# A two-layer graph kernel on one core: first two graphs' attention in four-pass products, first graph's side work divided anew

## The reference

```python
h = einsum('bni,oi->bno', x, W_fc)                    # 16 graphs, 512 nodes, 256 features; o = 32
f1, f2 = h @ a1, h @ a2                               # a1, a2: halves of W_attn
scores = leaky_relu(f1[:, :, None] + f2[:, None, :], 0.2)
attn = softmax(where(adj == 0, -1e9, scores), axis=2) # adj: 512 x 512 of 0/1 per graph
x = layernorm(x + elu(attn @ x))
xn = x / sqrt(max(sum(x * x), 1e-12))
x = layernorm(x + ((xn @ xn.T) @ adj) @ x)
```

## Time and profile before

| | |
|---|---|
| time, median of 3 runs (lowest to highest) | 339.91 us (339.04 to 342.74) |
| the profiled execution's own time | 339.95 us |
| its span, first to last instruction | 338.1 us |
| mean granted TensorE clock | 0.990 |
| busy: PE, PEld, DVE, ACT, POOL | 318.5, 301.3, 287.0, 293.3, 210.3 us |

### The profile page before, as it was taken

The page is one execution under the profiler, slowest core; times in us unless marked ns, Lnnn a source line. Parts: engine busy times, 40 slices in busy tenths (PEclk is TensorE's granted clock), DMA queues, the critical chain, the costliest instruction groups (busy, mean ns, idle before and its releaser), DMA issues.

```text
span 338.1 us, 7382 instructions
## 1 busy us (share of the span) xinstructions
PE 318.5 (94%) x2418; PEld 301.3 (89%) x2418; DVE 287.0 (85%) x1013; ACT 293.3 (87%) x610; POOL 210.3 (62%) x238
## 2 busy tenths in 40 slices
PE   6778899999989999999999999999999999999992
PEld 3577799989889999999999999999999998998881
DVE  2889999999788989989898989989898989856635
ACT  1589989999699999999999999999999999993561
POOL 4340493877447666675967676676958676665623
PEclk9979999999999999999999999999999999999998
DMA  8633461560715455264464454363464462210122
GB/s 237 201 88 104 123 186 25 166 186 8 240 37 156 124 151 163 71 181 124 126 181 130 127 157 156 81 186 111 138 174 128 131 177 67 65 62 0 44 73 74
DMA packets 33494, 41.93 MB, mean 124 GB/s; under 512 B 1168, under 2 KB 25264, under 8 KB 33456
## 3 DMA queue, kind: packets, MB, share of 16 engines
q0 software_dynamic: 16416, 24.64, 26.6%
q1 hardware_dynamic: 16944, 16.78, 15.9%
q10 hardware_dynamic: 96, 0.03, 0.0%
HBM read 33.06 MB, written 8.39 MB: 123 GB/s over the span
## 4 chain that ended last, share of the span: by engine, by line
PE 79%; DVE 10%; POOL 4%; issue 3%; ACT 2%; DMA 1%; POOLq 0%; ACTq 0%; DVEq 0%
PE ps_l L1208 14%; PE ps_l L1168 9%; PE ps_l L1169 8%; PE ps_h L1138 8%; PE ps_h L1139 7%; PE ps_h L1140 7%; PE ps_probT L1122 6%; PE ps_l L1194 4%; PE ps_l L1196 4%; PE ps_l L1195 4%; PE ps_l L1180 4%; PE ps_f L1111 2%; DVE score L453 1%; DVE product L432 1%; DMA wfc<-w_fc 1%
## 5 line engine op out<-in xcount | busy, mean ns | idle before, releaser
L1138 PE MATMUL ps_h<-x_hi,probT_hi 128*128 128x256 f32 x256 | 78.8, 308 | 7.6 <-POOL x_lo L263 2.3
L1139 PE MATMUL ps_h<-x_lo,probT_hi 128*128 128x256 f32 x256 | 72.0, 281 | 0.0
L1140 PE MATMUL ps_h<-x_hi,probT_lo 128*128 128x256 f32 x256 | 72.0, 281 | 0.0
L1168 PE MATMUL ps_l<-xn_hi,adj_sb 128*128 128x256 f32 x256 | 64.0, 289 | 0.8 <-POOL xn_lo L304 0.5
L1208 PE MATMUL ps_l<-w_sb,xnT 128*128 128x256 f32 x256 | 62.5, 380 | 0.8 <-ACT w_sb L873 0.6
L1169 PE MATMUL ps_l<-xn_lo,adj_sb 128*128 128x256 f32 x256 | 62.5, 283 | 0.0
L304 POOL TENSOR_TENSOR xn_lo<-xn,xn_hi 128x1024 fp32r<-128x1024 f32 x15 | 36.0, 2400 | 38.6 <-ACT xn_hi L843 38.6
L1138 PEld LDWEIGHTS ps_h<-x_hi,probT_hi 128*128 128x128 f32 x256 | 48.6, 190 | 12.1 <-DVE probT_lo L484 9.0
L798 ACT ACTIVATE score<-score,f 128x512 f32<-128x512 f32 x64 | 44.4, 726 | 8.7 <-DVE row_max L453 8.6
L1168 PEld LDWEIGHTS ps_l<-xn_hi,adj_sb 128*128 128x128 f32 x256 | 48.8, 191 | 2.4 <-DVE y L560 0.9
L1208 PEld LDWEIGHTS ps_l<-w_sb,xnT 128*128 128x128 f32 x256 | 45.1, 189 | 6.5 <-issue 1.9
(11 more groups left out here) (78 smaller groups left out, 794.9 us busy)
## 6 DMA issues: line engine op xcount, KB each, us to landing
adj_sb<-adj POOLq DMA_DIRECT2D x15, 1024.0 KB, 5.9
x_sb<-x SPq DMA_DIRECT2D x16, 512.0 KB, 4.7
x_hi<-x POOLq DMA_DIRECT2D x15, 512.0 KB, 4.1
out<-o_sb SPq DMA_DIRECT2D x15, 512.0 KB, 3.2
adj_sb<-adj POOLq DMA_DIRECT2D x4, 256.0 KB, 4.6
out<-o_sb SPq DMA_DIRECT2D x4, 128.0 KB, 1.7
wfc<-w_fc ACTq DMA_DIRECT2D x1, 32.0 KB, 3.8
attn_cols<-w_attn ACTq DMA_DIRECT2D x1, 0.2 KB, 2.9
```

Source lines behind the costliest of these rows:

```text
L1138: nc.tensor.matmul(ps, probT_hi[:, c, blk], x_hi[n][:, k, :], start=(k == 0), stop=False)
L1139: nc.tensor.matmul(ps, probT_hi[:, c, blk], x_lo[n][:, k, :], start=False, stop=False)
L1140: last = nc.tensor.matmul(ps, probT_lo[:, c, blk], x_hi[n][:, k, :], start=False, stop=(k == NC - 1))
L1168: nc.tensor.matmul(ps, a, xn_hi[n][:, k, :], start=(k == 0), stop=False)
```

## The change

Constants `WHOLE_P = 2` and `WHOLE_Z = 1`. For graphs below WHOLE_P, attend multiplies the unsplit probT and x, both float32, by one plain product for each block, as make_out does; DVE's probT_lo_part becomes a plain copy of the bank, ACT's probT_hi_part, x_hi's copy or load and x_lo are gone. For graph 0 (below WHOLE_Z) make_w multiplies unsplit z and xn, ACT writes z once and DVE's z_lo_part is gone. Graph 0's masks go from DVE to ACT, the sum of its y from DVE to POOL. wfc is loaded first on SP instead of second on ACT. The written-out lists of the first graphs, and a few steps of the last ones, have new orders.

```diff
@@ SP @@
+            sp.dma_start(wfc[:], w_fc).then_inc(wfc_in, 16)
             load_x(0)
@@ POOL @@
+            def residual_sum_part(c):
+                pool.wait_ge(q_ok, c + 1)
+                pool.tensor_tensor(y[0][:, c, :], y[0][:, c, :], exp_h[:, c, :], ALU.add).then_inc(y_ok, 1)
...
             load_adj(1)
-            split_x_part(0)
-            split_x_part(1)
-            split_x_part(2)
-            load_x_hi(1)
-            split_x_part(3)
-            split_x(1)
+            residual_sum_part(0)
             load_adj(2)
+            load_x_hi(2)
+            residual_sum_part(1)
+            residual_sum_part(2)
+            residual_sum_part(3)
+            load_x_hi(3)
             shifted_moments(0)
@@ DVE @@
             def probT_lo_part(g, c):
                 if not graph(g):
                     return
-                dve.wait_ge(probT_hi_ok, NC * g + c + 1)
+                if g < WHOLE_P:
+                    dve.wait_ge(probT_ps, NC * g + c + 1)
+                    if graph(g - 1):
+                        dve.wait_ge(h_ps, NC * (g - 1) + c + 1)
+                    nc.vector.tensor_copy(probT[:, c, :], ps_probT[c % 2][:]).then_inc(probT_ok, 1)
+                    return
...
@@ ACT @@
-            act.dma_start(wfc[:], w_fc).then_inc(wfc_in, 16)
...
+            def make_mask_part(c):
+                act.wait_ge(adj0_in[c], 16)
+                nc.scalar.activation(mask[:, c, :], adj_sb[0][:, c, :].bitcast(F32), ACT.Copy, bias=-MASKED,
+                                     scale=MASKED).then_inc(mask_ok, 1)
...
+                if g < WHOLE_Z:
+                    nc.scalar.activation(z_sb[:, c, :], ps_l1[(Z0 + c) % 3][:, 0:D], ACT.Copy,
+                                         scale=nrm[n][:, c:c + 1]).then_inc(z_ok, 1)
+                    return
...
             elu_exp(4, 1)
+            elu_relu(4, 1)
             make_mask(5)
             xn_hi_part(3)
-            elu_relu(4, 1)
@@ PE @@
+                    if g < WHOLE_P:
+                        last = nc.tensor.matmul(ps, probT[:, c, blk], x_sb[n][:, k, :], start=(k == 0),
+                                                stop=(k == NC - 1))
+                        continue
...
+                    if g < WHOLE_Z:
+                        last = nc.tensor.matmul(ps, z_sb[:, k, blk], xn[n][:, k, :], start=(k == 0),
+                                                stop=(k == NC - 1))
+                        continue
...
-            keep_warm(14)
+            keep_warm(8)
             bcast_f2(0)
-            keep_warm(24)
+            keep_warm(28)
             transpose_prob(0, 0)
             transpose_prob(0, 1)
+            transpose_prob(0, 2)
             attend(0, 0)
+            attend(0, 1)
             bcast_f2(1)
```

More of the change, by code:

```diff
@@ L235, in load_x_hi @@
             def load_x_hi(g):
[L236 removed]
+                if not graph(g) or g < WHOLE_P:
                     return
[L238 removed]
+                if g - NBUF >= WHOLE_P:
                     pool.wait_ge(h_ps, NC * (g - NBUF + 1))
[L240 removed]
+                    pool.wait_ge(x_lo_ok, g - NBUF - WHOLE_P + 1)
                 elif g == 1:
@@ L252, in split_x @@
             def split_x(g):
-                if not graph(g):
+                if not graph(g) or g < WHOLE_P:
                     return
@@ L636, in _ @@
             row_moments_part(3)
-            node_scores(2, 0)
-            masked_f2(2, 0)
             probT_lo_part(1, 2)
             probT_lo_part(1, 3)
+            node_scores(2, 0)
             normalise_part(0)
@@ L674, in _ @@
             masked_f2(3, 2)
+            masked_f2(3, 3)
+            probT_lo_part(2, 2)
+            probT_lo_part(2, 3)
             negate_max(3, 0)
-            residual(2)
-            residual2(0, 3)
-            z_lo_part(1, 0)
-            row_moments2(0)
+            negate_max(3, 1)
             z_lo_part(1, 1)
@@ L682, in _ @@
             z_lo_part(1, 3)
-            masked_f2(3, 3)
-            negate_max(3, 1)
+            node_scores(4, 1)
+            residual(2)
             probT_lo_part(3, 0)
@@ L939, in _ @@
-            elu_relu(1, 2)
             elu_exp(1, 3)
             elu_relu(1, 3)
+            scale_z(0, 0)
+            scale_z(0, 1)
+            lrelu(2, 0)
+            scale_z(0, 2)
             lrelu(2, 1)
-            scale_z(0, 0)
+            scale_z(0, 3)
+            copy_xnT(0, 0)
+            lrelu(2, 2)
+            copy_xnT(0, 1)
+            lrelu(2, 3)
             softmax_exp(2, 0)
             softmax_exp(2, 1)
-            scale_z(0, 1)
-            scale_z(0, 2)
-            scale_z(0, 3)
+            copy_w(0, 0)
@@ L949, in _ @@
+            copy_w(0, 1)
             probT_hi_part(2, 0)
-            copy_xnT(0, 0)
+            xn_hi_part(1)
             probT_hi_part(2, 1)
-            lrelu(2, 2)
-            lrelu(2, 3)
             softmax_exp(2, 2)
             softmax_exp(2, 3)
-            copy_xnT(0, 1)
-            copy_w(0, 0)
-            copy_w(0, 1)
+            make_mask(3)
+            scale_z(1, 0)
             probT_hi_part(2, 2)
             probT_hi_part(2, 3)
+            scale_z(1, 1)
+            lrelu(3, 0)
@@ L1022, in _ @@
             probT_hi_part(4, 3)
+            copy_xnT(2, 1)
             elu_exp(4, 0)
@@ L1242, in _ @@
             make_w(0, 1)
-            attend(2, 0)
+            transpose_prob(2, 0)
+            bcast_f2(3)
+            make_out(0, 0)
+            transpose_prob(2, 1)
+            make_out(0, 1)
+            make_out(0, 2)
+            make_out(0, 3)
             transpose_prob(2, 2)
             transpose_prob(2, 3)
-            bcast_f2(3)
-            attend(2, 1)
-            make_out(0, 0)
-            make_out(0, 1)
-            make_out(0, 2)
-            attend(2, 2)
-            attend(2, 3)
-            make_out(0, 3)
             make_z(1, 0)
@@ L1257, in _ @@
             make_z(1, 3)
+            attend(2, 0)
+            attend(2, 1)
+            attend(2, 2)
+            attend(2, 3)
             transpose_prob(3, 0)
+            transpose_xn(1, 0)
+            make_w(1, 0)
             transpose_prob(3, 1)
-            transpose_xn(1, 0)
             transpose_xn(1, 1)
-            make_w(1, 0)
+            transpose_prob(3, 2)
+            bcast_f2(4)
             make_w(1, 1)
-            transpose_prob(3, 2)
             transpose_prob(3, 3)
-            bcast_f2(4)
             for i in range(3, B - 2):
```

221 lines of the change are left out of this document (96 added, 125 removed).

## The result

The changed kernel takes 336.65 us (median of 4 runs, 336.09 to 337.11), the kernel before on the same chip 340.75 us (4 runs, 339.04 to 342.74): ratio 0.988, 95% interval [0.984, 0.993]. The forecast was 337.4 us (334.9 to 340.6), with within 1% of no change as the likeliest; the ratio's middle, 1.2% faster, lies just outside that. The profiled execution took 337.11 us with a span of 335.2 us, against 339.95 and 338.1. The experiments were run on three chips, on which the median of the kernel before was 339.53, 341.49 and 339.49 us, so times are compared on one chip where that is possible. One execution of the last kernel tried (456.45 us) ran wholly at a lower clock, and the comparison leaves it out.

What follows compares the result with a forecast made beforehand. Bound: a lead-in set by DVE and its chain of waits, then PE's serial work, then a tail. -5.0 + 0.6 + 0.3 + 1.4 + 0.1 = -2.6 from 339.95 gave 337.4 us, range 334.9 to 340.6.

Steps and rivals of the forecast that it cites:

- The frame: Whole kernel: DVE's chain sets make_z(0, 0), 5.0 us earlier; PE's work carries that to the end, except growth and stalls.
- First steps, -1.3: Lead-in up to masked_f2(0, 0): start at 9.85 us instead of 11.16, gain 1.3 us.
- To masked_f2(1, 0): Lead-in from masked_f2(0, 0): masked_f2(1, 0) at 19.3 us instead of 21.41, gain 2.1.
- To make_z(0, 0): Lead-in from masked_f2(1, 0): DVE's remaining list takes 14.9 us plus 0.4 for ACT's hop; make_z(0, 0) at 34.6.
- Whole make_w(0) +0.6: Graph 0's make_w on PE: 8 whole products at 0.08 us more each add 0.6 us.
- starts +0.3: PE from make_z(0, 0) to make_out(1, 0): 0.3 us taken for first-product starts.
- The late copy_xnT(2, 1), +1.4: ACT at graph 3 to 4: copy comes behind normalise2(1), make_out(2, 0) stalls 2.0 us instead of 0.6.
- mask(5), +0.1: ACT ahead of make_z(3, 0): one elu_relu, 0.35 us, now before mask(5), also freeing attend(4, 3); +0.1 us.
- Rival B: First attend of graph 0: clock falls to half, masked_f2(1, 0) 2.7 us late; 340.1 us, chance 0.16.
- Rival A: Graph 4: ACT runs ahead, so the late copy_xnT(2, 1) costs no more than before; 335.7 us, chance 0.32.
- C: Slower: half clock lasts beyond attend(0, 1), make_z(0, 0) at 40.6 us; 343.4 us, chance 0.07.
- D: Lead-in: POOL's sums of y wait for DMA issues, row_moments for them, only part gained; 339.3 us, chance 0.12.

Runs made afterwards that it cites:

- Experiments 3 and 4: Changed kernel with wfc second on ACT again: 338.72 us, ratio 0.995; kernel before with only wfc first on SP: 339.09 us, ratio 0.998.
- experiment 8: Changed kernel with 14 and 24 warming products, as before the change, in place of 8 and 28: 336.61 us, ratio 0.992.
- experiment 7: Changed kernel with graph 0's make_w split again (WHOLE_Z = 0), four z_lo on DVE between masked_f2 of graph 2: 336.99 us, ratio 0.988.
- experiment 1: Changed kernel with copy_w(2, 0) and copy_xnT(2, 1) ahead of normalise2(1) on ACT: 334.21 us, ratio 0.983.
- experiment 9: Kernel of experiment 1 with mask(5) ahead of elu_exp(4, 0) and xn_hi(3) ahead of elu_exp(4, 1) on ACT: 332.18 us, ratio 0.972.
- experiment 2: Changed kernel with 18 warming products in PE's wait ahead of make_out(2, 0), late copy_xnT(2, 1) left: 335.82 us, ratio 0.988.
- e8: Kernel of experiment 6: changed kernel with attend of graph 1 split again (WHOLE_P = 1): 340.43 us, ratio 0.995.
- e3: Changed kernel with wfc loaded second on ACT's queue again: 338.72 us, ratio 0.995.
- e7: Kernel of experiment 8: changed kernel with 14 and 24 warming products in place of 8 and 28: 336.61 us, ratio 0.992.
- e9: Kernel of experiment 7: changed kernel with make_w of graph 0 split again (WHOLE_Z = 0): 336.99 us, ratio 0.988.
- experiment 6: Changed kernel with attend of graph 1 split again (WHOLE_P = 1), x_hi(1), x_lo(1) and four probT_hi put back: 340.43 us, ratio 0.995.

## Why the prediction was right

The forecast was 337.4 us and -2.6 us. Measured are 336.65 us, -2.9 in the spans of the two profiled executions and -4.1 in the medians, whose 340.75 for the kernel before is 0.8 over the 339.95 that I counted from. That it came so close is in good part luck, since two errors nearly cancel.

- *The frame* (DVE's chain sets make_z(0, 0), then PE carries the shift to the end) holds: 229.2 and 229.1 us behind make_out(3, 0).
- *First steps, -1.3*: the mis-sized term. masked_f2(0, 0) came at 8.23, not 9.85: 2.9 us won. I took the earlier issue of wfc (0.45) and left its landing at 3.8 us; it landed after 2.0, so node_scores(0, 1) started at 5.45, not 7.03. Experiments 3 and 4 show that this is the move's doing: 1.5 to 1.75 us at masked_f2(0, 0). That the 14 warming products would then rule, and 8 not, was right (experiment 8).
- *To masked_f2(1, 0)*: counted 9.45 us, took 9.62. *To make_z(0, 0)*: counted 15.3, took 14.87. The lists of DVE's steps were the right tool.
- *Whole make_w(0) +0.6 and starts +0.3*: from make_z(0, 0) to make_out(1, 0) it is 29.35 against 28.65 before, +0.7. But the price isn't one of the whole product: in the new order the split costs 1.4 more (experiment 7), which a sum over PE alone can't see.
- *The late copy_xnT(2, 1), +1.4*: 1.94 in place of 0.56, exactly the step and the size that were foretold; experiment 1 takes it away.
- *mask(5), +0.1*: from mask(5)'s start to make_z(3, 0) it is 5.46 us before and 5.45 after, but PE comes to it 1.2 us sooner, so that its wait grew from 0.47 to 1.69; experiment 9 takes it away. PE's gap ahead of the fourth attend of graph 4 (0.8 us between starts beyond the usual 0.12) went in return, as I had said that elu_relu would free it: net +0.4 where I had +0.1.
- *Not foretold*: half clock behind the wait at make_out(2, 0), +1.6 in the profiled execution and in about half of all (experiment 2). Rival B had the mechanism, and put it at the first attend, where 1.00 was granted; it struck at the wait of which I had given the length. A stall was priced as its own length only, a term put at nothing without a reason.
- Rival A had the size (335.7 is 1.0 off, the forecast 0.75) and the wrong reason: ACT did not run ahead. C and D are refuted: 1.00 is granted from 10 to 40 us, and up to 40 us DVE has no wait for POOL, so its sums came in time.

From make_out(1, 0) to make_out(3, 0) the change lost 3.4 us (44.05 against 40.64) where I had +1.5: 1.4 by the longer wait for xnT, 1.6 by the clock and 0.4 by mask(5). make_z(0, 0) won 1.9 more than I had. The sum is right to 0.75 us, the two halves of it are each off by 1.9.

The Trainium skill, "TensorE: Matmul & The Clock Gate", section "HAM oscillation", tells of a kernel whose TensorE waits for data between bursts of products and comes back at the low clock every time. Behind the 1.94 us wait the profiled executions of the changed kernel and e8 agree (0.50 granted), and those of e3, e7 and e9 do not (1.00).

## What to carry to other kernels

Whole products in the old order were worth 0.8 us at make_z(0, 0) in the profiles, wfc's move 1.5 to 2, and all together with the new order 6.9; the new order without the whole products was not tried, so how much of the rest is its own is not shown. Where a lead-in is a chain of waits from engine to engine, take away a wait's cause and close up the lists in the same edit. A lead-in that gets shorter makes other waits late: after it, look again for the copy that PE waits for and for a mask that stands ahead of it in a list; here four lines moved in ACT's list (experiment 9) gave about as much again (ratio 0.988 to 0.972 and 0.978 on two chips) as the change itself (1 to 0.988). Price a PE wait of some 2 us at its length and, in about half of the executions, at 1 to 2 us more for the clock behind it.

## What the runs showed of the hardware that was not expected

- A small first load's landing depends on its queue and its place there, which these runs don't separate: wfc (32 KB) took 3.5 to 3.9 us as second load on ACT's queue in three profiled executions, 1.7 to 2.6 as first on SP's in eleven, and attn_cols (0.2 KB), which stayed on ACT, 2.7 to 3.1 against 1.6 to 1.9.
- A step of DVE can last as long as one of POOL: 2.57 us for 0.42 beside x_lo (experiment 6). Another case, in the changed kernel: a product that starts at 275.84 lasts 0.99 us and ends 0.29 us after POOL's x_lo (274.17, 2.37 us). The Trainium skill, "SBUF — State Buffer", section "Who interferes with whom", says that a DVE instruction with two SBUF inputs and a GpSimd one that reads SBUF exclude each other for a whole instruction; the traces agree, with both inputs of each in SBUF.
- A PE wait of about 2 us is followed by half clock in some executions and not in others of the same kernel (experiment 2: 19 of 37).
- The granted clock of a row can say 1.00 while products go at half the rate. In the stretch 7 to 10 us both the changed kernel and that of experiment 1 have PEclk 1.00, with 21 and 14 products; their 28 warming products last 3.59 and 4.74 us, and make_z(0, 0) comes 0.7 later in the second: there the transposes of graph 0 start right behind the warming products, at 12.45, and in the first they wait 0.21 us for prob and start at 11.67. In the five profiled executions in which the 28 last 4.45 to 4.74 us, attend(0, 0) starts 5.9 to 6.2 us behind masked_f2(0, 0), in the five in which they last 3.34 to 4.07 us, 5.4 to 5.5 behind.

```profile
7.00:10.00 3.00, 3.00 (x21) 2.61 (x22) 3.00 (x13) 2.64 (x5) 0.00 (x0) 1.00 1.04 301
```
```profile
7.00:10.00 3.00, 3.00 (x14) 2.33 (x15) 3.00 (x13) 2.57 (x5) 0.00 (x0) 1.00 1.14 328
```

Why the clock falls after the same wait in one execution and not in another stays open.
